# Attention on one core: a unit's probabilities-times-values product cut into four parts, one behind each step of a slot

## The reference

```python
dot = jnp.einsum('bqhs,bkhs->bhqk', queries, keys) * scale
att = jax.nn.softmax(dot, axis=-1)
out = jnp.einsum('bhqk,bkhs->bqhs', att, values).reshape(b, t, e)
return out @ Wu.T + bu
```

## Time and profile before

| | |
|---|---|
| Time, median of 3 runs | 1668.05 us (1664.76 to 1669.87) |
| Profiled execution, span | 1666.9 us |
| busy in the span: PE | 1519.7 us (91%) |
| VectorE (DVE) | 1383.8 us (83%) |
| ScalarE (ACT) | 920.8 us (55%) |
| GpSimd (POOL) | 296.9 us (18%) |

### The profile page before, as it was taken

The page is one execution under the profiler, slowest core; times in us unless marked ns, Lnnn a source line. Parts: engine busy times, 40 slices in busy tenths (PEclk is TensorE's granted clock), DMA queues, the critical chain, the costliest instruction groups (busy, mean ns, idle before and its releaser), DMA issues. The chain is left out here.

```text
span 1666.9 us, 24179 instructions
## 1 busy us (share of the span) xinstructions
PE 1519.7 (91%) x8562; PEld 759.0 (46%) x8562; DVE 1383.8 (83%) x2459; ACT 920.8 (55%) x1751; POOL 296.9 (18%) x364
## 2 busy tenths in 40 slices
PE   6899999999999999979997888976999869989699
PEld 2111111111111111268883333322888758869587
DVE  6999999999999999476664999999766657787686
ACT  3088888888888888832224765754322232222232
POOL 3200000000000000000013788784000200020000
PEclk7599999999999999989998999999999979999799
DMA  3340000100000001000001222220000003200123
GB/s 95 102 159 24 24 30 27 31 27 25 24 24 24 24 24 49 9 1 1 1 1 41 73 64 72 67 67 26 1 1 1 1 1 103 81 23 1 52 78 103
DMA packets 41315, 65.92 MB, mean 40 GB/s; under 512 B 11444, under 2 KB 18661, under 8 KB 40490
## 3 DMA queue, kind: packets, MB, share of 16 engines
q1 hardware_dynamic: 41194, 64.37, 12.6%
HBM read 56.68 MB, written 6.75 MB: 38 GB/s over the span
## 5 line engine op out<-in xcount | busy, mean ns | idle before, releaser
L844 DVE TENSOR_REDUCE row_max<-ps 128x1 f32<-128x1024 f32 x512 | 601.2, 1220 | 33.4 <-PE ps L641 17.4
L758 ACT ACTIVATE probs<-ps 128x512 f32<-128x512 f32 x944 | 487.8, 603 | 119.7 <-PE ps L656 119.4
L641 PE MATMUL ps<-k_stack,q_stack 48*128 48x512 bf16 x1024 | 325.0, 402 | 20.4 <-DVE row_max L844 10.6
L656 PE MATMUL ps<-q_stack,k_stack 51*128 51x512 bf16 x944 | 322.1, 387 | 2.2 <-ACT probs L758 0.2
L585 PE MATMUL ps<-probs,v_head 128*16 128x512 f32 x2048 | 269.8, 599 | 1.3 <-issue 1.1
L641 PEld LDWEIGHTS ps<-k_stack,q_stack 48*128 48x128 bf16 x1024 | 58.5, 95 | 368.0 <-DVE row_max L844 342.0
L1373 PE MATMUL ps<-s_hc,ident 128*128 128x512 f32 x256 | 139.0, 628 | 47.9 <-DVE s_hc L1646 42.9
L1026 ACT ACTIVATE x_gate<-ps 128x512 f32<-128x512 f32 x128 | 76.5, 599 | 184.5 <-PE ps L122 184.4
L1298 POOL TENSOR_TENSOR s_dbx<-s_dx,s_b_rows 128x512 f32<-128x512 f32 x128 | 159.4, 1270 | 35.2 <-DVE s_h L1637 34.7
L1637 DVE TENSOR_TENSOR_SCAN s_h<-ps,s_state,s_dbx 128x512 f32<-128x512 f32 x128 | 157.3, 1274 | 4.6 <-POOL s_dbx L1298 2.8
L1063 DVE TENSOR_TENSOR x_hidden<-x_gate,ps 128x512 f32<-128x512 f32 x128 | 87.2, 686 | 53.4 <-PE ps L122 42.5
(11 more groups left out here) (345 smaller groups left out, 1935.1 us busy)
## 6 DMA issues: line engine op xcount, KB each, us to landing
s_b_rows<-s_b_dram SPq DMA_DIRECT2D x64, 256.0 KB, 3.1
y_spread<-y_probs_dram SPq DMA_DIRECT2D x128, 128.0 KB, 2.9
q_stack<-q_parts_dram SPq DMA_DIRECT2D x30, 96.0 KB
k_stack<-k_parts_dram SPq DMA_DIRECT2D x30, 96.0 KB
w_w<-w_dram SPq DMA_DIRECT2D x1, 2048.0 KB, 8.0
q_stack<-q_parts_dram SPq DMA_DIRECT2D x30, 64.0 KB
k_stack<-k_parts_dram SPq DMA_DIRECT2D x30, 64.0 KB
o_dram<-o_sb SPq DMA_DIRECT2D x60, 32.0 KB
```

What stands on the lines that cost most here:

```text
L641: last = nc.tensor.matmul(core.ps[:, 2 * b + r, :], qst[buf][0:KROWS, u * P:(u + 1) * P], kst[buf][0:KROWS, key:key + CH], start=True, sto ...
L656: nc.tensor.matmul(core.ps[:, S_BANK + n % S_RING, :], kst[buf][HALF:ROWS, kt * P:(kt + 1) * P], qst[buf][HALF:ROWS, c * CH:(c + 1) * CH], ...
L758: nc.scalar.activation(probs[:, us % RING, c * CH:(c + 1) * CH], core.ps[:, S_BANK + n % S_RING, :], ACT.Exp).then_inc(exp_done, 1)
L844: nc.vector.tensor_reduce(mx[:, u, b:b + 1], core.ps[:, 2 * b:2 * b + 2, :], mybir.AxisListType.XY, ALU.max).then_inc(max_done, 1)
```

## The change

`weigh_values` can now do one of several parts of a unit: part p of 4 takes 128 of the 512 queries in each of the four column groups. In a slot, a part stands behind each pair of find and score. The first unit of a head stays whole, and stands behind the second pair. The wait for the unit's exponentials stands at the first part alone, the semaphore for the finished product at the last.

```diff
-            def weigh_values(m):
+            def weigh_values(m, part=0, of=1):
                 buf, kt = m // NT % NBUF, m % NT
-                if kt == 0:
-                    pe.wait_ge(v_staged, m // NT + 1)
-                    if m:
-                        pe.wait_ge(evacuated, m // NT)
-                pe.wait_ge(exp_done, 4 * m + 4)
+                if part == 0:
+                    if kt == 0:
+                        pe.wait_ge(v_staged, m // NT + 1)
+                        if m:
+                            pe.wait_ge(evacuated, m // NT)
+                    pe.wait_ge(exp_done, 4 * m + 4)
+                width = CH // of
+                cut = slice(part * width, (part + 1) * width)
                 for c in range(NC_):
-                    last = nc.tensor.matmul(core.ps[32 * c:32 * c + VROWS, O_BANK, :], v_head[buf][:, kt, :],
-                                            probs[:, m % RING, c * CH:(c + 1) * CH],
-                                            start=kt == 0, stop=kt == NT - 1)
-                last.then_inc(pv_done, 1)
+                    last = nc.tensor.matmul(core.ps[32 * c:32 * c + VROWS, O_BANK, cut], v_head[buf][:, kt, :],
+                                            probs[:, m % RING, c * CH:(c + 1) * CH][:, cut],
+                                            start=kt == 0, stop=kt == NT - 1 and part == of - 1)
+                if part == of - 1:
+                    last.then_inc(pv_done, 1)
...
                     if scores:
                         score(c)
-                if values:
-                    weigh_values(j * BODY + gs - LAG_V)
+                    if values and (gs - LAG_V) % NT == 0:
+                        if c == 1:
+                            weigh_values(j * BODY + gs - LAG_V)
+                    elif values:
+                        weigh_values(j * BODY + gs - LAG_V, c, 4)
```

## The result

The changed kernel takes **1712.41 us** (median of 4 runs, 1710.64 to 1714.85) against 1668.72 (4 runs): ratio 1.0272, 95% interval 1.0254 to 1.0290. It is slower by 44 us, where 38 were forecast (1706; range 1664 to 1765).

What follows compares the result with a forecast made beforehand. The loop was taken as bound by a ring through PE and ScalarE, 2.44 us a slot; after the split, PE at 2.64. 219 x 2.64 + 15 x 2.4 = 614 against 576 adds 38: 1706 us, range 1664 to 1765.

Steps and rivals of the forecast that it cites:

- VectorE's floor: Attention loop: two reductions, the second starting 1.14 us after the first, let VectorE alone do a slot in 2.28 us.
- the ring through PE and ScalarE: Old slot: find and score, exponential, bank wait, third later score, product: 0.49 + 0.60 + 0.05 + 0.32 + 0.98 = 2.44 us.
- The price of a change of shape: On PE, each change between row-tiled scores and column-tiled product costs 0.09 to 0.10 us, on either side.
- the step: Split slot: one find, score and part on PE take 0.32 + 0.34 = 0.66 us, four steps 2.64.
- The 0.12 of a part: Part's time beyond two passes of 0.11 us: second pass's load, spacing of groups, change back; called likeliest to be wrong.
- the rival held likeliest for a much larger loss: PE cannot issue so densely: at 0.085 us a matmul-load pair a slot takes 3.4, total 1870 us; chance 0.12.
- The rival of hidden changes: Next tile shape's loads run ahead during streaming: step 0.45 us, VectorE the bound, total 1632 us; chance 0.12.
- The 1.05 from L1354 to the next L1356: Old trace: L1356 starts 1.05 us after its own two passes of 0.86; cited as a change's cost without a wait.
- The sum: Loop's 234 slots: 576 us before, 219 x 2.64 + 15 x 2.4 = 614 after; 38 us added.
- VectorE's slack: VectorE waits for PE in the split loop; its end-of-head work, 0.46 us once a head, falls into that slack.
- The whole unit, 2.4: Slot of a head's first, unsplit unit, which waits for the head's output copy: 2.4 us, bounds 2.0 and 2.6, 15 slots.
- One sign: Changed profile, ScalarE: its wait for scores was to grow from 77 us.

Runs made afterwards that it cites:

- runs with two blocks: Against the kernel before: two 256-query parts 1637.92 us; four parts in pairs behind steps two and four 1634.05; two parts, head's first unit behind step four 1631.08.
- three runs with 32 matmuls a unit: Changed kernel with its four parts placed together after step four, 1673.52 us; in three blocks, 1667.71 us; in pairs behind steps two and four, 1634.05 us.
- three blocks: Changed kernel with one part behind the first step, one behind the second, two behind the fourth: 1667.71 us, ratio 1.0005 to the kernel before.

## Why the prediction was right

**What bounds the kernel.** Right: the loop was not at VectorE's floor, and the ring through PE and ScalarE held it 0.16 above. The runs with two blocks reach 2.26, against 2.28 read from the earlier trace rows.

**The price of a change of shape.** Right in cause and size. 0.32 and 0.34 were forecast for the two sides of a part and 0.66 for the step; the trace shows 0.32, 0.34 and 0.66. The 0.12 of a part, named as the likeliest error, held at a quarter of the product's size. A pass over 128 queries does take 0.11: 32 matmuls in one place take 1.00 and 8 take 0.34, so six passes more take 0.66. Then 0.34 - 2 x 0.11 leaves 0.12 for a part, as 0.98 - 0.86 does for a whole product. The three runs with 32 matmuls a unit and two, six and four changes separate the changes from the number of instructions, which was the rival held likeliest for a much larger loss. The rival of hidden changes falls too: the 0.32 stands ahead of the parts without a wait of their own as well as ahead of the others.

One figure of the prediction needs a second look. The 1.05 from L1354 to the next L1356 is 0.19 over 0.86 of streaming, not 0.10. The single records put L1354's two passes at 900.584 and 901.118, 0.53 apart, so 0.10 of the 0.19 lies between them and 0.09 at the change behind the second.

A rival that the prediction doesn't name is the type of the numbers: scores are bf16 and products f32, so each change of shape is also one of type. The timeline of PE in the kernel before has a change of type alone, in the scan (L1373 f32, two passes, 128 rows deep; L1366 bf16, 96 rows; both across all columns):

```profile
923.63 1.02 PE L1373 MATMUL ps<-s_hc,ident 128*128 128x512 f32 x2
924.49 0.38 PE L1366 MATMUL ps<-s_bc,w_pick 96*128 96x512 bf16 x1
924.71 1.02 PE L1373 MATMUL ps<-s_hc,ident 128*128 128x512 f32 x2
```

They follow each other after 0.86, two passes' streaming, and 0.22, one bf16 matmul's: the type costs nothing there. And the earlier trace rows have 0.09 for a change of rows without one of type. What PE does in the 0.10 us of a change no run shows.

**The sum.** 7.7 us too small in the loop of the profiled execution, which ends 45.7 us later by the first score of the tail (its line's first start is 708.4 us instead of 662.7), where 38 were forecast; the medians differ by 44. Two terms account for nearly all of it. The step is 0.664 rather than 0.66, a slot 2.655 instead of 2.64: 219 x 0.015 = 3.3. And a head's disturbances don't fall wholly into VectorE's slack, as the text had it. The slot behind a whole unit takes 2.81, 0.15 over the others. The rest of the difference between heads, 42.47 - 15 x 2.655 - 2.39 - 0.15 = 0.10, lies in the slot in which VectorE joins the maxima (L854 starts at 327.04), where one find waits for VectorE:

```profile
328.01 0.09 PEld L645 LDWEIGHTS ps<-k_stack,q_stack 48*128 48x128 bf16 x1 [0.21 <-issue]
...
328.78 0.09 PEld L645 LDWEIGHTS ps<-k_stack,q_stack 48*128 48x128 bf16 x1 [0.32 <-DVE row_max L851]
```

It comes 0.77 behind the find before it, 0.11 over a step. So of the 0.46 that the work at a head's end takes, all but 0.11 did fall into the slack. Together 15 x 0.25 = 3.8. The whole unit, 2.4, is right at 2.39.

**What would show it.** One sign failed. ScalarE was to wait longer than 77 us for scores; the list shows 9. Many of its waits, some 0.06 each, are too short for the list, but they are not longer in sum either: by its busy time ScalarE stands idle 54 of the 520 us, where it was 77 before. Four exponentials in close order took 2.07 with one wait of 0.38; apart, each takes its whole 0.60 of a step of 0.66. That VectorE waits, 0.19 twice a slot where about 0.3 a slot was forecast, is seen in the timeline alone.

## What to carry to other kernels

A product that is put into an engine's gaps pays for every border that it makes: count the changes of the array's shape in a slot, price one from a place where such a change stands without a wait, and cut no finer than the gaps need. Here two blocks a slot gain 1.7 to 2.1%, three change nothing and four lose 2.7%, at the same arithmetic. When three engines look full, look for a ring before believing any of them: two neighbouring instructions that follow without a wait give an engine's floor, and mean durations don't (1.13 to 1.14 against 1.22 for VectorE here).

## What the runs showed of the hardware

A change between row-tiled scores and column-tiled products costs PE 0.09 to 0.10 us at a granted clock of 1.00, also where nothing is waited for: a score starts 0.23 behind another, and a product 0.32 behind a score; with three blocks instead of four, two changes less, a slot is 0.23 shorter.

Dense small matmuls cost less than was allowed for: 32 matmuls of 128 queries with their 32 loads pass in 1.00 us, 31 ns each, where four column groups run side by side.
